# GpSimd's preparation work cut into pieces with a budget per step, values loaded earlier and ahead of the bias, in an AdaLN transformer layer on Trainium2

## What is computed

```python
h = _layernorm(x, axis=-1) * (1 + ca) + sa
x = x + ga * attn(h, ...)
h = _layernorm(x, axis=-1) * (1 + cb) + sb
x = x + gb * ffn(h, ...)      # router, top 2 of 8 experts

# attn: B = 2, T = 2048, D = 256, H = 16 heads of 16
scores = sips_alpha[0] * jnp.tanh(raw / sips_beta[0])       # raw = q k^T
hamming = jnp.einsum('bid,bjd->bij', soft_bits, soft_bits) / 2.0   # soft_bits = tanh(x @ hex_w.T)
scores = scores + lam * hamming[:, None, :, :]
lat = jnp.einsum('bid,hde,bje->bhij', hexc, Mh, hexc) / 6.0        # hexc = tanh(x @ q6_w.T)
scores = scores + lat * (jax.nn.sigmoid(scale_logit) * 2.0)
scores = jnp.where(causal[None, None], scores, -jnp.inf)
attn = jax.nn.softmax(scores, axis=-1)
out = jnp.einsum('bhij,bhjd->bhid', attn, v) ... @ out_w.T
```

## Time and profile before

| | |
|---|---|
| median of 3 runs | 1891.63 us (1886.49 to 1897.06) |
| the profiled execution | 1886.52 us |
| its span in the trace | 1884.8 us |
| attention loop in the trace | about 95 to 1213 us |
| PE, DVE, ACT, POOL busy | 92%, 69%, 65%, 33% of the span |

### The profile page before, as it was taken

The page is one execution under the profiler, slowest core; times in us unless marked ns, Lnnn a source line. Parts: engine busy times, 40 slices in busy tenths (PEclk is TensorE's granted clock), DMA queues, the critical chain, the costliest instruction groups (busy, mean ns, idle before and its releaser), DMA issues. The chain is left out here.

```text
span 1884.8 us, 35364 instructions
## 1 busy us (share of the span) xinstructions
PE 1742.2 (92%) x11140; PEld 1042.5 (55%) x11141; DVE 1307.1 (69%) x2675; ACT 1232.5 (65%) x1260; POOL 618.5 (33%) x715
## 2 busy tenths in 40 slices
PE   4787999999999988999999999899659999999997
PEld 1343434343333333433433334388449999999997
DVE  6466878888878866878877778644546666666664
ACT  1175999999989967889999999733513333333332
POOL 0643352434325243351240202127612222222222
PEclk8777999999999989999999999999869999999998
DMA  4687695767763178686566770172257777777773
GB/s 163 178 214 163 164 198 134 171 107 155 151 129 97 61 155 212 136 175 140 136 128 127 170 135 21 48 239 75 91 183 204 198 197 196 197 196 196 199 204 79
DMA packets 183563, 288.50 MB, mean 153 GB/s; under 512 B 20832, under 2 KB 114144, under 8 KB 181280
## 3 DMA queue, kind: packets, MB, share of 16 engines
q1 hardware_dynamic: 168096, 264.92, 55.4%
q0 software_dynamic: 13440, 17.97, 5.7%
q10 hardware_dynamic: 1920, 4.23, 0.6%
HBM read 218.09 MB, written 68.96 MB: 152 GB/s over the span
## 5 line engine op out<-in xcount | busy, mean ns | idle before, releaser
L1217 DVE SCALAR_TENSOR_TENSOR probs<-probs,scal,bil_ps 128x512 f32<-128x512 f32 (+1 forms) x1152 | 789.5, 714 | 258.0 <-PE bil_ps L1059 206.4
L1138 ACT ACTIVATE probs<-probs 128x2048 f32<-128x2048 f32 (+1 forms) x288 | 522.7, 1815 | 100.9 <-DVE probs L1217 100.1
L1131 ACT ACTIVATE probs<-raw_ps 128x2048 f32<-128x2048 f32 (+1 forms) x288 | 509.0, 1767 | 28.9 <-PE raw_ps L1041 18.4
L1059 PE MATMUL bil_ps<-u_mv,w_st 50*128 50x512 f32 (+3 forms) x1280 | 466.5, 456 | 17.6 <-DVE probs L1217 14.7
L1059 PEld LDWEIGHTS bil_ps<-u_mv,w_st 50*128 50x128 f32 x1280 | 199.4, 189 | 502.3 <-DVE probs L1217 416.0
L1939 ACT ACTIVATE rows_sb<-fc_ps,b 128x128 f32<-128x128 f32 x576 | 160.7, 368 | 345.7 <-DVE hid_lo L1971 304.7
L1078 PE MATMUL o_ps<-probs,v_sb 128*32 128x512 f32 (+3 forms) x2560 | 302.2, 554 | 23.5 <-POOL probs L897 12.9
L1041 PE MATMUL raw_ps<-q_mv,k_st 64*128 64x512 f32 (+3 forms) x1280 | 272.6, 395 | 10.7 <-ACT probs L1131 9.6
L1895 PE MATMUL fc_ps<-modrow,rows_sb 128*128 128x128 f32 x2304 | 271.5, 276 | 0.0
L1895 PEld LDWEIGHTS fc_ps<-modrow,rows_sb 128*128 128x128 f32 x2304 | 265.5, 193 | 0.0
L1868 POOL DMA_INDIRECT out<-modrow,token x72 | 125.2, 1738 | 380.1 <-DVE modrow L2004 362.9
(11 more groups left out here) (233 smaller groups left out, 1537.6 us busy)
## 6 DMA issues: line engine op xcount, KB each, us to landing
rows_sb<-in_w SPq DMA_DIRECT2D x72, 1024.0 KB, 4.9
q_mv<-q_split SPq DMA_DIRECT2D x128, 128.0 KB, 7.5
k_st<-k_split SPq DMA_DIRECT2D x48, 256.0 KB, 8.6
rows<-x_rows SPq DMA_DIRECT2D x72, 130.0 KB, 2.1
v_rows<-rows_sb SPq DMA_DIRECT2D x8, 1024.0 KB, 7.9
o_t<-o_sb SPq DMA_DIRECT2D x32, 256.0 KB, 8.0
k_st<-k_split SPq DMA_DIRECT2D x16, 512.0 KB, 8.4
v_sb<-v_rows SPq DMA_DIRECT2D x8, 1024.0 KB, 14.3
```

What stands on the lines that cost most here:

```text
L1059: mm = pe.matmul(bil_ps[:, hd % 2, column:column + width], codes(kt)[row:row + BIAS_ROWS, :], u_mv[row:row + BIAS_ROWS, p, hd // 2, query: ...
L1131: act.activation(probs[:, s % NBUF, :, first:BLK], raw_ps[:, :, first:BLK], ACT.Tanh).then_inc(tanh_ready, 1)
L1138: act.activation(scores, scores, ACT.Exp).then_inc(exp_ready, 1)
L1217: dve.scalar_tensor_tensor(scores, scores, scal[:, ALPHA:ALPHA + 1], bil_ps[:, hd % 2, first:BLK], ALU.mult, ALU.add).then_inc(sum_ready, 1)
```

## The change

1. POOL's jobs get a list `POOL_JOBS`, planned ahead: `split_codes` is cut into four pieces, `split_lattice` into two, `weigh` into one per k, the router split into four. Each piece has an assumed cost in `COST`. Each step has room for 1.9 on the diagonal and 3.4 elsewhere; the first job of a step goes in even where it is over the room, except that off a short block a job above 2.4 is not put on a diagonal step.
2. SP's stores follow the pieces (`STORE_AT`: one or two steps behind the job) and stand behind the codes, keys and bias loads of their turn.
3. Values: blocks with 3 or 7 steps per iteration use the lower half of a `v_sb` buffer for head groups 0 and 1 and the upper half for 2 and 3, so that four iterations are held; there are four semaphores `values_in`. `VALUES_FREE[it]` is the last iteration that used the same place. Loads of such iterations come one iteration earlier, and `load_values` is the first load of its turn, ahead of codes, keys and bias.
4. The output projection of blocks 0, 1, 2, 4, 5, 6 moves back by 2 to 10 steps (`step = load + LANDING + (3 if i else 7)`, `loadable = step + 4`), and the second norm with it.

```diff
-    step = load + LANDING + 2
+    step = load + LANDING + (3 if i else 7)
...
-    loadable = step + 2
...
+    loadable = step + 4
...
+COST = {"codes": (1.9, 2.2, 1.3, 3.2), "lattice": (3.2, 1.9), "heads": (1.9,), "guard": (3.4,), "norm": (2.0,) * TPB,
+        "gate": (1.3,), "share": (1.25,) * KC, "ln": (2.3, 2.9, 2.2, 2.4, 2.4), "split": (1.0, 2.3) * 2}
...
+    pending = sorted(pending + fresh, key=lambda job: URGENT.get(job[0], 0))
+    room = 1.9 if s in DIAG else 3.4
+    while pending:
+        kind, i, n = pending[0]
+        cost = COST[kind][n % len(COST[kind])]
+        short = BLOCKS[ITERS[STEPS[s][0]][0]][1] == 0
+        if cost > room and (s in POOL_JOBS or s in DIAG and cost > 2.4 and not short):
+            break
+        POOL_JOBS.setdefault(s, []).append(pending.pop(0))
...
-VALUES_AT = {LAST[it - 2] + 1: it for it in range(2, len(ITERS))}
+def values_row(it):
+    i, g = ITERS[it]
+    return T // P // 2 * (g // 2) if BLOCKS[i][1] < NBLK // 2 else 0
...
+VALUES_FREE = {it: max([before for before in range(it) if values_used(before) & values_used(it)], default=-1)
+               for it in range(len(ITERS))}
+VALUES_AT = {}
+for it in range(2, len(ITERS)):
+    VALUES_AT.setdefault(max(LAST[VALUES_FREE[it]] + 1 if VALUES_FREE[it] >= 0 else 0, LAST[it - 3] + 1 if it > 2 else 0),
+                         []).append(it)
...
-                for i, o in DONE_AT.get(s - POOL_LAG - 1, []):
-                    store(i, o)
+                for it in VALUES_AT.get(s, []):
+                    load_values(it)
                 if s in CODES_AT:
                     load_codes(CODES_AT[s])
...
-                if s in VALUES_AT:
-                    load_values(VALUES_AT[s])
+                for i, o in STORE_AT.get(s, []):
+                    store(i, o)
...
-            split_codes(0)
...
+                for kind, i, n in POOL_JOBS.get(s, []):
+                    piece(kind, i, n)
```

More of the change, by code:

```diff
@@ L177 @@
 ROWS_FREE = CLOSES[N_BLK - 1] + POOL_LAG + 4
-SPLIT_AT = {}
-for part in range(2):
-    SPLIT_AT[min(s for s in range(ROWS_FREE + 4, NSTEP) if s not in DIAG and s not in LN_AT and s not in SPLIT_AT)] = part
-BACK_AT = {max(max(SPLIT_AT) + 4, max(s for s, i in H2_AT.items() if i == N_BLK - 3) + 2): (0, N_BLK - 2),
-           H2_DONE: (N_BLK - 2, N_BLK - 1)}
+COST = {"codes": (1.9, 2.2, 1.3, 3.2), "lattice": (3.2, 1.9), "heads": (1.9,), "guard": (3.4,), "norm": (2.0,) * TPB,
+        "gate": (1.3,), "share": (1.25,) * KC, "ln": (2.3, 2.9, 2.2, 2.4, 2.4), "split": (1.0, 2.3) * 2}
@@ new lines @@
+URGENT = {"gate": 1, "share": 1, "norm": 1, "ln": 2, "split": 3}
+PIECE_OF = {"C": "codes", "L": "lattice", "G": "guard"}
+POOL_JOBS, JOB_DONE = {}, {}
+pending = []
+for s in range(NSTEP):
+    fresh = []
+    for i, o in DONE_AT.get(s - POOL_LAG, []):
+        if o in PIECE_OF:
+            fresh += [(PIECE_OF[o], i, n) for n in range(len(COST[PIECE_OF[o]]))]
+        elif o[0] == "Q":
+            fresh.append(("heads", i, int(o[1])))
+    fresh += [("norm", i, t) for i, t in NORM_AT.get(s, [])]
+    if s in SHARE_AT:
+        fresh += [("share", SHARE_AT[s], k) for k in range(KC)]
+        if SHARE_AT[s] % NBLK == 0:
+            fresh.insert(0, ("gate", SHARE_AT[s], 0))
+    if s in LN_AT:
+        fresh.append(("ln",) + LN_AT[s])
+    if s == ROWS_FREE + 4:
+        fresh += [("split", 0, n) for n in range(4)]
+    pending = sorted(pending + fresh, key=lambda job: URGENT.get(job[0], 0))
[7 more added lines that the diff above has]
+        POOL_JOBS.setdefault(s, []).append(pending.pop(0))
+        JOB_DONE[kind, i, n] = s
+        room -= cost
@@ new lines @@
+assert not pending
+LAST_JOB = {"C": ("codes", 3), "L": ("lattice", 1), "G": ("guard", 0)}
+STORE_AT = {}
+for s in DONE_AT:
+    for i, o in DONE_AT[s]:
+        if o == "V1":
+            STORE_AT.setdefault(s + POOL_LAG + 1, []).append((i, o))
+        elif o in LAST_JOB or o[0] == "Q":
+            kind, n = LAST_JOB.get(o, ("heads", int(o[1]) if o[0] == "Q" else 0))
+            if (kind, i, n) in JOB_DONE:
+                STORE_AT.setdefault(JOB_DONE[kind, i, n] + 1 + (i > EARLY), []).append((i, o))
@@ L183 @@
+H2_AT = {JOB_DONE["ln", i, NORM_PARTS - 1] + 1: i for i in OUTS}
+LAST_SPLIT = JOB_DONE["split", 0, 3]
+BACK_AT = {max(LAST_SPLIT + 2, max(s for s, i in H2_AT.items() if i == N_BLK - 3) + 2): (0, N_BLK - 2),
+           max(H2_AT) + 2: (N_BLK - 2, N_BLK - 1)}
 SLOTS_W = 5
@@ L527, in stage_front @@
         bias_in = [sem(f"bias_in{p}") for p in range(2)]
-        values_in = [sem(f"values_in{p}") for p in range(2)]
+        values_in = [sem(f"values_in{p}") for p in range(4)]
         codes_in = sem("codes_in")
@@ L907, in gate_weights, with weigh @@
                                    ).then_inc(wo_ready, 1)
-            def weigh(i):
-                pool.wait_ge(o_back, 16 * 2 * KC * (i + 1))
-                for k in range(KC):
-                    pool.tensor_tensor(num[:, k, :], num[:, k, :], inv_w[:, k, :], ALU.mult).then_inc(share_ready, 1)
-                pool.wait_ge(share_ready, KC * (i + 1))
+            def weigh(i, k):
+                if k == 0:
+                    pool.wait_ge(o_back, 16 * 2 * KC * (i + 1))
+                pool.tensor_tensor(num[:, k, :], num[:, k, :], inv_w[:, k, :], ALU.mult).then_inc(share_ready, 1)
+                if k == KC - 1:
+                    pool.wait_ge(share_ready, KC * (i + 1))
             def second_norm(i, part):
```

149 lines of the change are left out of this document (82 added, 67 removed).

## The result

The changed kernel runs in 1880.5 us (median of 8 runs, 1875.4 to 1883.8) where the kernel before, in 8 runs beside it, took 1891.4 (1884.4 to 1897.1). The ratio is 0.9945, 95% interval 0.9925 to 0.9965: faster by 10.9 us, 0.55%. Forecast were 1857 and a gain of 34.5. The sign is right; two thirds of the gain are missing, and the time is outside the range (1846 to 1874). The profiled execution has a span of 1874.3 us against 1884.8, 10.5 less, so what is missing must show in it. Both profiled executions lie 4 to 5 us under the median of their kernel.

The account below looks back on a forecast made before the run. ACT was taken to bound the loop, PE close behind. Stops costing 43.5 us, less 9 that stay, gave 34.5 saved: from the median 1891.6 to a forecast of 1857 us, range 1846 to 1874.

Parts of the forecast that it names:

- The five stops and their price: Three PE waits for POOL's mask, two for values loads; price 43.5 us over iterations 3, 4, 14, 18 and 20.
- Part 1: POOL's jobs in pieces: a mask is late by at most 0.9 us, inside its room, so the mask stops go.
- the 2.8 us of room: At step 8, how late POOL may be: 4.0 us of room, of which the mask takes 1.2.
- Rival (b): POOL's budget fails and masks stay late by 1 us at three places: 12 us lost, 1869; chance 0.08.
- Part 2: Values of iterations 3 and 20 go out about 14 and 20 us earlier, land before use; both stops go.
- Part 3: Values ahead of the bias, at iterations 4 and 20: keys late by 0.6 to 1.5 us, bias by 1 to 4.
- What would make me wrong beyond: Further signs of error: DVE waiting on a head split, or a stop in SP's queue behind a late store.
- Part 4: What stays at the borders and short iterations: 5 with the gates, 3 and 1, together 9 us (3 to 20).
- rival (a): Waits move to the loads: each border loses 8 to 10 us, inner short iterations 4; 1872 to 1874; chance 0.18.
- Its sign: A PE stop above 4 us at the first raw scores or bilinear sums of iterations 4 and 20.
- Rival (c): Bias late behind values in all eight short iterations: 48 us lost against 43.5 gained, 1896; chance 0.05.
- Part 5: Output projection 2 to 10 steps later, last second norm by step 281 instead of 278: costs nothing.

Follow-up runs that it names:

- experiment 2: Kernel before with only the new values scheme (buffer rows, semaphores, earlier loads), POOL's work as it was: 1886.0 us, ratio 0.9990.
- experiment 4: Changed kernel with DVE's reciprocal of block 4's denominators at step 168 instead of 164, its store later too: 1866.6 us, ratio 0.9888 to the kernel before.
- 12: Changed kernel with the reciprocal four steps later, run a second time beside the changed kernel on one chip: 1867.5 us, ratio 0.9877 to the kernel before.
- experiment 8: Kernel before with the values scheme and the later reciprocal, without POOL's pieces: 1879.5 us, ratio 0.9935.
- experiment 3: Changed kernel with the values load directly behind the bias load of its turn: 1885.2 us, ratio 0.9965 to the kernel before.
- 5: Changed kernel with the load of the denominators ahead of the bias in its turn: 1874.7 us, ratio 0.9906 to the kernel before.
- 11: The changed kernel once more, unaltered, on one chip with other runs: 1884.0 us, ratio 0.9949 to the kernel before.
- 9: Experiment 4 with the load of block 4's input rows in turn 20 instead of 3: 1869.3 us, ratio 0.9884 to the kernel before.
- 10: Experiment 4 with block 4's rows loaded in turn 20 and the gates at step 22 instead of 9: 1883.0 us, ratio 0.9955 to the kernel before.
- 6: Changed kernel with values behind the bias and block 4's reciprocal four steps later: 1871.9 us, ratio 0.9898 to the kernel before.
- 7: Experiment 4 with only 128 of 1024 key columns loaded for iteration 20, 0.9 MB less: 1862.0 us, ratio 0.9844 to the kernel before.

## Why the prediction was wrong in size and right in sign

**The five stops and their price: right.** All five are gone. Where nothing new came in their place, the iteration gained what was worked out: 7.0 of 7.7 in iteration 14, 8.3 of 9.8 in 18, and 7.8 of 8.0 in iteration 20 with the values alone (experiment 2). That a stop costs more than its length also held for the new one: 7.79 us of PE's stop, 13.0 of the iteration, at a clock of 0.78.

**Part 1, the pieces: right.** No mask is late in either profile of the changed kernel, as the 2.8 us of room said, and DVE waits for no head split. Rival (b) did not occur. One small cost was not on the list: a piece that runs beside DVE's work, 1.2 us in iteration 24 (last section).

**Parts 2 and 3, what is late next: this step failed.** Both values stops go, as Part 2 says. But Part 3 asks what is late next of keys and bias only, the loads of the attention itself, and the sum gives every other load a lateness of nothing, without a reason. DVE's in-order wait for the denominators was on no list. The trace of before held what was needed: load issued 748.80, landed 6.4 us later, used at 762.15, with an idle SP ahead of it that the removed stop had caused. The load had 13.4 us from issue to use; with 9.8 to 14.5 us to land in a full queue, the wait was there to be suspected. It was 8.00 us and cost 13 us of iteration 21; experiments 4 and 12 take both away, and experiment 8 the 8.3 us of experiment 2. It is no coincidence of this chip or run: experiments 2, 3, 5 and 11 have it too. "What would make me wrong beyond" named DVE as the engine, but a head split as the cause.

**Part 4, what stays at the borders: mis-sized.** Of 9 us, 5 were for the first border and 4 for iterations 18 to 20. Iterations 3 and 4 took 47.5 us against 36.4 of their like, so 11.1 stay; iterations 18 to 20 56.0 against 46.9 (10.5, 10.5 and 25.9), so 9.1 stay. Together 20.2, the upper bound (20) and not the value taken. The stops of 3.13, 2.80 and 4.68 us are those that Part 3 named, keys and bias. Of its lateness, the 1 to 4 us for the bias hold at the first border (2.80) and not at the second (4.68), and the 0.6 to 1.5 for the keys was too small: PE asked for them 7.3 us behind the end of iteration 2 (Part 3 has 7.7), but they landed 10.4 behind it, where Part 3 has 8.3 to 9.2, by their landing time in the old kernel. The gates, whose stop Part 4 takes as the least that stays at the first border, cost nothing there beside keys and bias (experiments 9 and 10: 45.8 us with them, 46.3 without).

This is rival (a), which had 8 to 10 us a border: right in mechanism, and near in size. Its sign was met at iteration 20 (4.68, above 4) and not at 4. Its 1872 to 1874 lacked the 13 us, and is not its own sum either: two borders of 8 to 10 and 4 more leave 19.5 to 23.5 of 43.5, which is 1868 to 1872. The lower end of the range mixes two bases in the same way: 1846 is taken from the profiled execution, and from the median, as the forecast, it would be 1851.

The sum by what was measured: 43.5 - 20.2 - 13.0 = 10.3, against 10.5 in the span. The terms not named above (-1.3 to 1.0 each) cancel. It is the sum of one execution. In the second profile of the changed kernel (1883.9 us) iterations 2 to 4 stand 18.8 us above their like, with waits for keys and bias in iteration 2 too, and 18 to 20 stand 13.8 above, while iteration 1 ends 5.2 us earlier than before. So what stays at the borders differs by more than 10 us between two executions of one kernel; what iteration 21 loses does not (12.8 there).

**Part 3, order: wrong in its reason.** Values ahead of the bias does delay the bias (experiment 3: iteration 20 26.4 without it, 33.2 and 31.5 with it), but moving it back gains nothing in all (3 and 6). What limits there is bytes (7). Rival (c) did not occur: iteration 17 is at 10.4 in both profiles. Iteration 19 is at 10.9 in one and at 16.2 in the other, where it waits for keys (3.70 us) and not for the bias.

**Part 5: nearly right.** The stretch from the loop's end to the span's end, 671.4 us before, is 670.4 after. But in iteration 12 the later second norm puts seven small instructions of its statistics on DVE right behind block 2's reciprocal and ahead of the next score sum (463.75 to 464.60). PE has a stop of 0.74 to 0.77 us there in every kernel with the pieces and the later output projection, and none above 0.7 without; the iteration takes 57.0 us instead of 56.1. This is read from the traces, not tested.

**The version that beats both** is experiment 4, the change with the reciprocal later: 1866.6 and 1867.5 us, 0.988 of the kernel before and 14 to 17 us below the changed kernel. Against the pieces alone (1873.6, same chip), the values part brings 7 us once its wait is out of the way, and none with it (0.9927 for the pieces alone, 0.9945 and 0.9949 for the whole change).

**What stays open.** The iterations 0 to 4 of one kernel end at different times from run to run (182.0 and 185.5 in the changed kernel, 185.5 and 182.8 in experiment 4), and iteration 19 of both has two lengths (10.9 and 16.2; 10.6 and 14.8); why was not found. A gain of 3 us at the first border can't be told from this, and whether fewer bytes would pay there was not settled. Iteration 15 is 0.9 us longer in every kernel with the pieces and in none without; why was not tested.

## What to carry to other kernels

In this kernel a stop on the critical engine also drained the DMA queue and gave slack to the loads behind it. Before forecasting that a stop's whole price comes back, list each wait that an in-order engine on the path has for a DMA, small ones too, with its slack (use less landing), and take the landing time of a full queue. Where the loads are more than the queue moves in the time, as at the second border here, reordering them changed who waits; give a wait slack by placing its instruction later, or move fewer bytes.

## What the runs showed of the hardware

Block 4's load of 32 KB landed in 6.4 us where SP had issued nothing for 7.4 us shortly before, and in 9.8 to 18.7 us in the other kernels. Block 3's, of the same size, landed in 2.2 us before (at 690, DMA share 0.59) and in 6.0 us after (at 672, share above 1). Issuing can take long too: one store held SP's queue for 7.24 us (at 735.75, above), where two others of its line took 0.65 and 0.70 (705.69 and 712.73), and another kind 8.88 us (experiment 3, at 712.16), where the next of it took 0.71; the DMA share in these two stretches was 0.74 and 0.93.

The runs of experiment 4 lie within 3.8 and 4.6 us (four each), the changed kernel's within 8.4 (eight) and 19 (ten). That the wait makes the spread is not shown: the numbers of runs differ.

A small instruction of DVE can be held by POOL. Timelines of DVE and POOL in experiment 4, and PE's next stop; the same DVE instruction took 0.17 us at 467.63, with no POOL work beside it:

```profile
809.27 0.98 DVE L514 TENSOR_SCALAR ln<-ln 128x4 f32<-128x4 f32 x1
```

```profile
808.96 1.26 POOL L920 TENSOR_TENSOR work<-work 12x512 f32<-12x512 f32 x1
```

```profile
811.77 0.49 PE L1141 MATMUL bil_ps<-u_mv,w_st 50*128 50x512 f32 x1 [1.69 <-DVE probs L1299]
```

The same place before the change:

```profile
832.61 0.50 PE L1059 MATMUL bil_ps<-u_mv,w_st 50*128 50x512 f32 x1 [0.48 <-DVE probs L1217]
```

The DVE instruction ended at 810.25, when POOL's ended (810.22). The Trainium skill (SBUF — State Buffer, Who interferes with whom) says that the two engines share a pair of ports that one instruction holds to its end, and the trace agrees. It is not free: this one and the next but one (0.57 us instead of 0.17, beside a CAST of POOL) put off the score sum behind them by 1.2 us, and PE's stop there grew by 1.2, from 0.48 to 1.69. POOL's L920 is a piece of the code split; both holds and the stop are in every kernel with the pieces and in none without, and iteration 24 takes 45.1 us after the change instead of 43.8.
